# Attention kernel, token stage: inverses of the softmax row sums spread by GpSimd and turned as two 128x128 squares; VectorE's norm and maximum placed between the two statistics instructions of a row

## The chip, the cores and the metric

The kernel runs on one core of one Trainium2 chip. The metric is the time of one execution in microseconds (us), lower is better. TensorE is written PE in the profile (PEld is its loading of weights), VectorE DVE, ScalarE ACT, GpSimd POOL, the queue of the sync engine SP.

## The reference

Three layers are computed on 4 samples of 32x32 pixels with 256 channels (1024 tokens of 256 values each). The middle one is a Nystrom attention with 8 heads of 32 channels and 128 landmarks, and it is there that the change acts:

```python
kernel_1 = softmax(einsum('bhnd,bhmd->bhnm', q, k_l))   # tokens x landmarks
kernel_2 = softmax(einsum('bhmd,bhld->bhml', q_l, k_l)) # landmarks x landmarks
kernel_3 = softmax(einsum('bhmd,bhnd->bhmn', q_l, k))   # landmarks x tokens
pinv = _iterative_pinv(kernel_2)                        # 6 iterations
attn = kernel_1 @ (pinv @ (kernel_3 @ v))
t = t + attn @ w_out.T + b_out                          # attn on _ln_t(t)
t = t + _L1_ffn_ref(_ln_t(t), ...)                      # 16 experts, top 2
```

Ahead of it stands a plain attention over the pixels of a sample, behind it a layer norm and a mixture of 16 experts.

## The kernel before, in words

Everything is in float32. The samples are passed through one after another (variable `i`, 4 passes). A pass has three stages of 8 units each (`UNITS = 3 * NT` = 24, `NT` = 8 row tiles of 128): units 0 to 7 are the plain attention, 8 to 15 the landmark rows with the iterated inverse, 16 to 23 the token stage, which holds `kernel_1` and is where the change acts. After the four passes come the routing and 79 blocks of the experts.

Each engine has its own program, written out by hand; engines meet only at counting semaphores. No scheduler or planner orders the work: what stands first in an engine's code runs first, and an engine that waits holds up all that stands behind it. In the token stage every engine loops over steps `s` = 0 to 9; a tile `t` passes through several steps.

- PE, step `s`: `turn_probs(s)` (8 transposes of the exponentials of tile `s`, L530), `scores(s+2)` (L633), `values(s-1)` (8 matmuls onto 32 partitions each, four column strips of the array side by side, L709), `turn_inverses(s)` (L683), `finish(s-2)` (L723, the output projection). Towards the end stand also transposes of the next sample's input (`turn(16)`, `turn(20)`), and its projections `project_tpg` (L559).
- ACT, step `s`: the exponentials of tile `s+1`, one instruction for each head with the row's sum (L1053), then the copy of the turned exponentials of tile `s` out of PSUM (L1061).
- DVE, step `s`: `inverses(s)` (reciprocal of 8 row sums, L1303), `rows1(s-3)` (adds the residual, L1358, then the two statistics instructions L1324 and L1326 through `moments`), `norm1(s-4)` (L1329), `maxima(s+2)` (L1206), `out_t(s-1)` (L1320), `inverses_turned(s)` (L1307).
- POOL: for each tile, the power -1/2 of the variance (`deviation`, L391 and L392), which `norm1` waits for.

The softmax of `kernel_1` is divided out late. The outputs of `values` have channels on partitions and tokens along the row, so the reciprocals (tokens on partitions, 8 heads along the row) must be turned as well: `turn_inverses` multiplies with `ident`, taking one head's column of `head_inv` 32 times as the weights; 8 matmuls fill PSUM with [32 equal rows for each head x 128 tokens]. `inverses_turned` copies this to `inv_T`, and `out_t` multiplies by it. `turn_inverses(s)` and `values(s-1)` write two halves of one PSUM bank, so `out_t(s-1)` waits for `turn_inverses(s)` (semaphore `inv_mm`). The first waits of `finish(s-2)` are `ot_ready` (from `out_t`) and `pr_used`, which `rows1(s-3)` raises when it has read the bank of the projection.

At the end of a pass DVE has to give the next pass its start as well: `phi_out` (L1212) for the projections, `bulk` (L1194) copies, and `maxima(0)` of the next pass.

Of the kernel before, what the change touches and what calls it, by code (L numbers as in the profile page):

```python
# [5 lines left out]
P = 128  # L6
# [12 lines left out]
QUADS = 4  # L19
# [27 lines left out]
def conv_attn_nystrom_moe_kernel(  # L47
# [34 lines left out]
    with ExitStack() as ctx:  # L82
# [57 lines left out]
        head_inv = sb("head_inv", [P, 2, HEADS])  # L140
        neg_max = sb("neg_max", [P, 2, NT])
# [79 lines left out]
        dve_steps = Chain(sem("dve_steps"), 44)  # L221
# [32 lines left out]
        inv_mm = sem("inv_mm")  # L254
        inv_copied = sem("inv_copied")
# [6 lines left out]
        x2_done = sem("x2_done")  # L262
        dev_ready = sem("dev_ready")
# [104 lines left out]
        def _(pool):  # L368
# [37 lines left out]
            for i in range(B):  # L406
                for t in range(NT + 1):
                    if t < NT:
                        pool.wait_ge(x1_done, i * NT + t + 1)
                        apart(pool, "pool")  # L410
                        deviation(t, i).then_inc(dev_ready, 1)
                    if t >= 1:
                        pool.wait_ge(xn_ready, i * NT + t)
                        pool.tensor_tensor(x1[:, t - 1, :], x1[:, t - 1, :], bo1, ALU.add).then_inc(x1b_ready, 1)
                if i + 1 < B:
                    add_bias(i + 1)
                for t in range(NT):
                    pool.wait_ge(x2_done, i * NT + t + 1)
                    apart(pool, "pool")
                    deviation(t, i).then_inc(dev2_ready, 1)  # L420
                pool_steps.close()
# [112 lines left out]
        def _(pe):  # L534
# [125 lines left out]
            for i in range(B):  # L660
# [13 lines left out]
                def turn_inverses(t):  # L674

                    pe.wait_ge(inv_ready, i * NT + t + 1)
                    if t == 0:

                        pe.wait_ge(pr_used, i * UNITS + 2 * NT)
                    for g in range(NG):  # L680
                        for j in range(QUADS):
                            h = g * GH + j
                            mm = pe.matmul(PS[HD * j:HD * j + HD, 0, g * P:(g + 1) * P], head_inv[:, t % 2, PLACE[h]:PLACE[h] + 1].broadcast_to([P, HD]),  # L683
                                           ident[:], start=True, stop=True, tile_position=(0, HD * j))
                    mm.then_inc(inv_mm, 1)
# [479 lines left out]
        def _(dve):  # L1165
# [128 lines left out]
            for i in range(B):  # L1294
                link = lambda ins: dve_steps.link(dve, ins, i)

                def inverses(t):

                    u = 2 * NT + t
                    dve.wait_ge(s_exp, i * UNITS + u + 1)  # L1300
                    if t >= 2:
                        dve.wait_ge(inv_mm, i * NT + t - 1)
                    dve.reciprocal(head_inv[:, t % 2, :], head_sum[:, u % 2, :]).then_inc(inv_ready, 1)  # L1303
# [47 lines left out]

                def rows1(t):
# [6 lines left out]
                    dve.wait_ge(pr_used, i * UNITS + u + 1)  # L1359
                    apart(dve, "dve")  # L1360
                    moments(t2_row(t), t, x2_done)
# [134 lines left out]
                for s in range(NT + 2):  # L1496
                    if 1 <= s < NT:
                        inverses(s)
                    if s == 0:
# [10 lines left out]
                    if s >= 3:  # L1510
                        rows1(s - 3)
                    if s >= 4:
                        norm1(s - 4)
                    if s + 2 < NT:
                        maxima(2 * NT + s + 2)
                    if 1 <= s < NT:
                        out_t(2 * NT + s - 1)
# [5 lines left out]
                if more:  # L1523
                    phi_out(i + 1, 1)
                norm1(NT - 2)
                if more:
                    bulk(18, xT[:, 0, 0:512])
                    maxima(0, i + 1)
# [166 lines left out]
```

## Time and profile before

| | |
|---|---|
| median of 3 runs | 1000.76 us (999.5, 1000.76, 1002.37) |
| the profiled execution, its own time | 999.48 us |
| its span | 997.3 us |
| PE busy | 908.4 us (91%) |
| PE weight loads busy | 699.0 us (70%) |
| DVE busy | 569.3 us (57%) |
| ACT busy | 448.1 us (45%) |
| POOL busy | 298.6 us (30%) |
| granted PE clock, mean | 0.956 of full speed |
| chain that ended last | PE 73%, DVE 13%, issue 5%, DMA 4%, ACT 3%, POOL 1% |

The span reaches from the first to the last instruction; what lies around it is 2.2 us. The chain is followed back from the last instruction to what released each step. Busy times of matmuls overlap one another, so it is starts that tell the pace: the token stage of the second sample runs from about 293 to 334 us, and those of the others lie at about 138, 444 and 599 us.

### The profile page before, as it was taken

The page shows a single profiled execution, that of the slowest core. Times are in us where ns is not written, and L with a number is a line of the kernel's source. Part 1 is how long each engine was busy: PE and PEld are TensorE (multiplying, and loading weights), DVE is VectorE, ACT ScalarE, POOL GpSimd, SP SyncE. Part 2 cuts the span into 40 slices and gives each one's busy share as a digit, 9 for nine tenths or more (in the row PEclk, how much of TensorE's full clock was granted, in tenths as well). Part 3 has the DMA queues.
Part 4 walks back from the last instruction along what each step waited for, and adds up shares of the span by engine and source line. Part 5 has one row for each costly group of instructions (what it writes and reads, how often), then busy time and mean ns, then how long its engine had stood idle before and what let it go on. Part 6 is the DMA issues. An engine that isn't in the chain of part 4 may idle for free.

```text
span 997.3 us, 21748 instructions
## 1 busy us (share of the span) xinstructions
PE 908.4 (91%) x6980; PEld 699.0 (70%) x6982; DVE 569.3 (57%) x1585; ACT 448.1 (45%) x1004; POOL 298.6 (30%) x343
## 2 busy tenths in 40 slices
PE   5999989899999899999899999546899999999997
PEld 3565767565767565767556767335789999999996
DVE  3478857587857687866678866693222222222221
ACT  1424367433359443349443348253334444444442
POOL 3050001060001050001130000103467666767664
PEclk9699999899999999999899999857999999999999
DMA  3100000300000300000200000499444444444341
GB/s 106 43 2 1 1 2 23 107 1 1 2 1 2 126 3 1 2 1 2 86 1 1 1 2 2 135 252 326 125 67 71 66 69 66 69 65 64 62 65 16
DMA packets 47848, 50.76 MB, mean 51 GB/s; under 512 B 11073, under 2 KB 41153, under 8 KB 47777
## 3 DMA queue, kind: packets, MB, share of 16 engines
q0 software_dynamic: 15168, 18.85, 11.7%
q1 hardware_dynamic: 32608, 30.99, 10.3%
q8 instruction: 42, 0.69, 0.3%
q14 instruction: 30, 0.24, 0.1%
HBM read 33.00 MB, written 18.78 MB: 52 GB/s over the span
## 4 chain that ended last, share of the span: by engine, by line
PE 73%; DVE 13%; issue 5%; DMA 4%; ACT 3%; SPq 1%; POOL 1%; POOLq 0%; DVEq 0%; ACTq 0%
PE PS L982 12%; PE PS L530 11%; PE PS L991 11%; PE PS L851 7%; PE PS L559 6%; PE PS L622 4%; PE PS L723 3%; PE PS L633 3%; PE PS L704 3%; DVE neg_max L1206 3%; DMA out_dram<-low,row_of 3%; PE PS L627 3%; PE PS L709 2%; ACT arena L1053 1%; PE PS L718 1%
## 5 line engine op out<-in xcount | busy, mean ns | idle before, releaser
L391 POOL TENSOR_SCALAR aggr<-aggr 128x1 f32<-128x1 f32 x64 | 14.3, 223 | 519.6 <-DVE aggr L1326 519.6
L1206 DVE TENSOR_REDUCE neg_max<-PS 128x1 f32<-128x1024 f32 (+1 forms) x96 | 117.5, 1224 | 78.2 <-PE PS L633 27.4
L530 PE MATMUL PS<-ident,arena 128*128 128x128 f32 x1008 | 140.3, 287 | 19.8 <-DMA arena<-in_x_dram 6.9
L982 PEld LDWEIGHTS PS<-low 128*128 128x128 f32 x1264 | 155.1, 194 | 4.1
L530 PEld LDWEIGHTS PS<-ident,arena 128*128 128x128 f32 x1008 | 122.7, 150 | 46.9 <-issue 37.7
L982 PE MATMUL PS<-low 128*128 128x128 f32 x1264 | 155.3, 277 | 0.0
L991 PE MATMUL PS<-arena,low 128*128 x632 | 151.9, 384 | 3.3 <-issue 1.6
L439 POOL DMA_INDIRECT out_dram<-low,row_of x79 | 125.4, 1588 | 87.0 <-DVE low L1660 38.6
L1061 ACT COPY arena<-PS 128x1024 f32<-128x1024 f32 x96 | 98.4, 1025 | 92.0 <-PE PS L530 92.0
L991 PEld LDWEIGHTS PS<-arena,low 128*128 128x128 f32 x632 | 114.9, 192 | 18.0 <-issue 5.4
L1149 ACT ACTIVATE low<-PS 128x512 f32<-128x512 f32 x79 | 47.2, 597 | 156.6 <-PE PS L982 156.6
L1048 ACT ACTIVATE arena<-PS,neg_max 128x1024 f32<-128x1024 f32 x64 | 71.3, 1114 | 97.0 <-DVE neg_max L1206 97.0
L425 POOL DMA_INDIRECT low<-rows_scratch,token_of x79 | 78.3, 991 | 65.9 <-DVE token_of L1616 39.4
L1660 DVE TENSOR_SCALAR low<-PS,slot_gate 128x256 f32<-128x256 f32 x79 | 38.2, 483 | 99.8 <-issue 65.0
L1140 ACT COPY low<-arena 128x1024 f32 x79 | 82.5, 1045 | 28.2 <-issue 28.2
L1053 ACT ACTIVATE arena<-PS,neg_max 128x128 f32<-128x128 f32 x256 | 90.4, 399 | 7.6 <-DVE neg_max L1206 7.6
L1641 DVE TENSOR_TENSOR gate_parts<-low,pick_of 128x2 f32<-128x2 f32 x79 | 12.7, 161 | 129.6 <-PE PS L530 129.6
L851 PE MATMUL PS<-arena 128*128 128x256 f32 x320 | 74.4, 386 | 0.0
L559 PE MATMUL PS<-arena,low 128*128 128x512 f32 x128 | 63.6, 622 | 4.5 <-DVE arena L1460 2.6
L851 PEld LDWEIGHTS PS<-arena 128*128 128x128 f32 x320 | 59.1, 190 | 11.2 <-issue 4.0
L1053 ACT ACTIVATION_READ_ACCUMULATOR arena<-PS,neg_max 128x1 f32 x256 | 60.9, 238 | 0.0
L1025 ACT ACTIVATE arena<-PS 128x512 f32<-128x512 f32 x40 | 23.7, 596 | 81.9 <-PE PS L559 40.2
(203 smaller groups left out, 1312.2 us busy)
## 6 DMA issues: line engine op xcount, KB each, us to landing
arena<-in_L_ffn_W_dram SPq DMA_DIRECT2D x32, 512.0 KB, 5.7
arena<-in_x_dram SPq DMA_DIRECT2D x4, 1024.0 KB, 6.4
out_dram<-t SPq DMA_DIRECT2D x4, 1024.0 KB, 6.8
rows_scratch<-arena SPq DMA_DIRECT2D x4, 512.0 KB, 3.7
rows_scratch<-arena SPq DMA_DIRECT2D x8, 256.0 KB, 2.6
low<-rows_scratch,token_of POOLq DMA_INDIRECT x79, 2.9
out_dram<-low,row_of POOLq DMA_INDIRECT x79, 3.8
arena<-in_L_attn_w_qkv_dram SPq DMA_DIRECT2D x1, 768.0 KB, 4.8
```

Source lines behind the costliest of these rows:

```text
L425: pool.indirect_dma_start(xg[:, n % 4, :], None, rows_dram, bass.IndirectOffsetOnAxis(ap=token_of[:, n:n + 1], axis=0)).then_inc(xg_loaded ...
L439: pool.indirect_dma_start(out_rows, bass.IndirectOffsetOnAxis(ap=row_of[:, n:n + 1], axis=0), y_sb[:, n % 4, :], None, bounds_check=T - 1, ...
L530: mm = pe.transpose(PS[0:s.shape[1], dst_bank, n * P:n * P + s.shape[0]], s, ident[0:s.shape[0], 0:s.shape[0]])
L559: mm = pe.matmul(PS[0:m, bank, :], w[c], src[:, c, half * 512:half * 512 + 512], start=c == 0, stop=c == KC - 1)
L851: mm = pe.matmul(bank[:, o:o + 2 * M], RX[:, g, h, 0, :], RX[:, g, h].rearrange("p r m -> p (r m)"), start=True, stop=True)
L982: mm = pe.matmul(PS[:, 2 + p, hc * P:(hc + 1) * P], w1_now[:, p, c * H + hc * P:c * H + (hc + 1) * P], xgT[:, p, c, :], start=c == 0, stop ...
L991: mm = pe.matmul(PS[:, 6 + p, 0:D], hT[:, p, c, :], w2_sb[:, bass.ds(e * (HC * D) + c * D, D)], start=c == 0, stop=c == HC - 1)
L1048: act.activation(Pm[:, u % 2, :], src, ACT.Exp, bias=neg_max[:, u % 2, 0:1], accum_out=row_sum[:, u % NT:u % NT + 1]).then_inc(s_exp, 1)
L1053: ins = act.activation(Pm[:, u % 2, o:o + M], src[:, o:o + M], ACT.Exp, bias=neg_max[:, u % 2, h:h + 1], accum_out=head_sum[:, u % 2, h:h ...
L1061: act.copy(PT[:, u % 2, :], PS[:, 2:4, :].rearrange("p b n -> p (b n)")).then_inc(t_act, 1)
L1140: act.copy(w1_now[:, p, :], w1_sb[:, bass.ds(e * (KC * H), KC * H)]).then_inc(w1_staged, 1)
L1206: dve.tensor_reduce(dst, src, AX.X, ALU.max, negate=True).then_inc(s_max, 1)
```

## The change

Two parts.

1. `turn_inverses` no longer multiplies. A new buffer `inv_spread` (128 x 2 x 256) is filled by POOL (`spread_inverses`): two copies per tile write each head's reciprocal 32 times side by side. PE then turns the two 128x128 squares with two transposes. POOL waits for `inv_ready`, PE for the new semaphore `inv_spread_ready`, and `inverses(t)` waits for POOL's reading of tile `t-2`. POOL's `deviation(t-3)` stands behind `spread_inverses(t)`.
2. On DVE the row statistics are taken apart: `rows1` only adds, `stats1` and `moments1` are functions of their own. In a step `rows1` and `norm1` come first, then `stats1`, `maxima`, `moments1`; `bulk(20)` and the last `out_t` now stand behind `rows1` and `norm1`, and in the last steps `phi_out` stands ahead of `stats1`.

```diff
+                def spread_inverses(t):
+                    pool.wait_ge(inv_ready, i * NT + t + 1)
+                    if t >= 2:
+                        pool.wait_ge(inv_mm, i * NT + t - 1)
+                    by_place = head_inv[:, t % 2, :].rearrange("p (a g b) -> p g a b", g=NG, b=2)
+                    for g in range(NG):
+                        pool.tensor_copy(inv_spread[:, t % 2, g * P:(g + 1) * P].rearrange("p (a b d) -> p a b d", a=2, b=2),
+                                         by_place[:, g].unsqueeze(3).broadcast_to([P, 2, 2, HD])).then_inc(inv_spread_ready, 1)
+
+                for t in range(NT + 3):
+                    if t < NT:
+                        spread_inverses(t)
+                    if t >= 3:
+                        pool.wait_ge(x2_done, i * NT + t - 3 + 1)
+                        apart(pool, "pool")
+                        deviation(t - 3, i).then_inc(dev2_ready, 1)
...
-                    pe.wait_ge(inv_ready, i * NT + t + 1)
+                    pe.wait_ge(inv_spread_ready, (i * NT + t + 1) * NG)
-                    for g in range(NG):
-                        for j in range(QUADS):
-                            h = g * GH + j
-                            mm = pe.matmul(PS[HD * j:HD * j + HD, 0, g * P:(g + 1) * P], head_inv[:, t % 2, PLACE[h]:PLACE[h] + 1].broadcast_to([P, HD]),
-                                           ident[:], start=True, stop=True, tile_position=(0, HD * j))
-                    mm.then_inc(inv_mm, 1)
+                    transposes(pe, 0, [inv_spread[:, t % 2, g * P:(g + 1) * P] for g in range(NG)]).then_inc(inv_mm, 1)
...
                 for s in range(NT + 2):
                     if 1 <= s < NT:
                         inverses(s)
+                    if s >= 3:
+                        rows1(s - 3)
+                    if s >= 4:
+                        norm1(s - 4)
...
                     if s >= 3:
-                        rows1(s - 3)
-                    if s >= 4:
-                        norm1(s - 4)
+                        stats1(s - 3)
                     if s + 2 < NT:
                         maxima(2 * NT + s + 2)
+                    if s >= 3:
+                        moments1(s - 3)
```

The order on DVE in a middle step of the token stage (from the reciprocal to `out_t`; `t2` holds the rows after the attention, and `arena` in the norm is the buffer `xn`), before:

```order
L1303 RECIPROCAL head_inv<-head_sum 128x8 [waits inv_mm,s_exp]
L1358 TENSOR_TENSOR t2<-PS,arena 128x256 [waits x1b_ready,pr_mm]
L1324 BN_STATS stats<-t2 128x6 [waits pr_used]
L1326 BN_AGGR aggr<-stats 128x2 [waits dve_steps]
L1329 TENSOR_SCALAR arena<-t2,aggr 128x256 [waits dev2_ready]
L1206 TENSOR_REDUCE neg_max<-PS 128x8 [waits s_exp,s_mm]
L1320 TENSOR_TENSOR low<-PS,arena 128x256 [waits inv_copied,inv_mm,pr_mm,pv_mm]
```

and now:

```order
L1315 RECIPROCAL head_inv<-head_sum 128x8 [waits inv_spread_ready,s_exp]
L1380 TENSOR_TENSOR t2<-PS,arena 128x256 [waits x1b_ready,pr_mm]
L1341 TENSOR_SCALAR arena<-t2,aggr 128x256 [waits dev2_ready]
L1367 BN_STATS stats<-t2 128x6 [waits pr_used]
L1218 TENSOR_REDUCE neg_max<-PS 128x8 [waits s_exp,s_mm]
L1372 BN_AGGR aggr<-stats 128x2 [waits x2_stats]
L1332 TENSOR_TENSOR low<-PS,arena 128x256 [waits inv_copied,inv_mm,pr_mm,pv_mm]
```

The norm has moved ahead of the statistics, and the maximum between the two statistics instructions; nothing is added or taken away.

On PE at the same step, from `values` to `finish`, before:

```order
L709 MATMUL PS<-arena,low 32x128 [waits inv_copied,ot_ready,t_act]
L709 MATMUL PS<-arena,low 32x128 x7
L683 MATMUL PS<-ident,head_inv 32x128 [waits inv_ready]
L683 MATMUL PS<-ident,head_inv 32x128 x7
L723 MATMUL PS<-low 128x256 [waits pr_used,ot_ready]
L723 MATMUL PS<-low 128x256
```

and now:

```order
L721 MATMUL PS<-arena,low 32x128 [waits inv_copied,ot_ready,t_act]
L721 MATMUL PS<-arena,low 32x128 x7
L547 MATMUL PS<-ident,inv_spread 128x128 [waits inv_spread_ready]
L547 MATMUL PS<-ident,inv_spread 128x128
L735 MATMUL PS<-low 128x256 [waits pr_used,ot_ready]
L735 MATMUL PS<-low 128x256
```

The eight matmuls onto 32 partitions are two transposes onto 128, and they wait for POOL in place of DVE.

On POOL, for two tiles in the middle of the stage, now (before, only the pairs on `aggr` stood there):

```order
L428 COPY inv_spread<-head_inv 128x128 [waits inv_mm,inv_ready]
L428 COPY inv_spread<-head_inv 128x128
L394 TENSOR_SCALAR aggr<-aggr 128x1 [waits x2_done]
L395 TENSOR_TENSOR aggr<-aggr,minus_half 128x1 [waits pool_steps]
L428 COPY inv_spread<-head_inv 128x128 [waits inv_mm,inv_ready]
L428 COPY inv_spread<-head_inv 128x128
```

The two copies of a tile stand behind the deviation that the step before asked for, and ahead of the one of its own step.

On DVE at the end of the stage, from the last-but-one `out_t` on, before:

```order
L1320 TENSOR_TENSOR low<-PS,arena 128x256 [waits inv_copied,inv_mm,pr_mm,pv_mm]
L1307 COPY arena<-PS 128x256 [waits inv_mm]
L1194 COPY arena<-PS 128x512 [waits bulk_mm]
L1320 TENSOR_TENSOR low<-PS,arena 128x256 [waits inv_copied,pr_mm,pv_mm]
L1358 TENSOR_TENSOR t2<-PS,arena 128x256 [waits x1b_ready,pr_mm]
L1324 BN_STATS stats<-t2 128x6 [waits pr_used]
L1326 BN_AGGR aggr<-stats 128x2 [waits dve_steps]
L1329 TENSOR_SCALAR arena<-t2,aggr 128x256 [waits dev2_ready]
```

and now:

```order
L1332 TENSOR_TENSOR low<-PS,arena 128x256 [waits inv_copied,inv_mm,pr_mm,pv_mm]
L1319 COPY arena<-PS 128x256 [waits inv_mm]
L1380 TENSOR_TENSOR t2<-PS,arena 128x256 [waits x1b_ready,pr_mm]
L1341 TENSOR_SCALAR arena<-t2,aggr 128x256 [waits dev2_ready]
L1206 COPY arena<-PS 128x512 [waits bulk_mm]
L1332 TENSOR_TENSOR low<-PS,arena 128x256 [waits inv_copied,pr_mm,pv_mm]
L1367 BN_STATS stats<-t2 128x6 [waits pr_used]
L1372 BN_AGGR aggr<-stats 128x2 [waits x2_stats]
```

The addition L1358 (now L1380), which raises `pr_used`, stood behind the copy of 512 and the last `out_t`; now it stands ahead of both, and the norm directly behind it.

## Rows read from the trace of the kernel before

**Rows 1.** Chain that ended last, second sample, a middle step: start us, us, what

```profile
311.71 0.57 PE PS L709 x16
312.29 0.44 PE PS L683 x16
312.72 1.06 PE PS L723 x4
313.78 0.87 PE PS L530 x8
314.66 1.06 PE PS L633 x8
```

**Rows 2.** Timeline, DVE, same step: start us, us, engine, line, operation [idle before <-releaser]

```profile
311.76 1.22 DVE L1206 TENSOR_REDUCE neg_max<-PS 128x8 f32<-128x1024 f32 x1 [0.33 <-PE PS L633]
...
312.90 0.41 DVE L1320 TENSOR_TENSOR low<-PS,arena 128x256 f32<-128x256 f32 x1
...
313.56 0.19 DVE L1303 RECIPROCAL head_inv<-head_sum 128x8 f32<-128x8 f32 x1
...
314.39 0.43 DVE L1324 BATCH_NORM_STATS2 stats<-t 128x6 f32<-128x256 f32 x1
...
314.96 0.18 DVE L1326 BATCH_NORM_AGGREGATE aggr<-stats 128x2 f32<-128x6 f32 x1
...
315.77 1.22 DVE L1206 TENSOR_REDUCE neg_max<-PS 128x8 f32<-128x1024 f32 x1 [0.33 <-PE PS L633]
```

**Rows 3.** Timeline, ACT, second sample: first exponential of two tiles that follow each other

```profile
301.26 0.44 ACT L1053 ACTIVATE arena<-PS,neg_max 128x128 f32<-128x128 f32 x1
...
305.00 0.40 ACT L1053 ACTIVATE arena<-PS,neg_max 128x128 f32<-128x128 f32 x1
```

**Rows 4.** POOL: a copy of 128x128 (ns min/median/max), and the deviation's second instruction (timeline)

```profile
L405 POOL COPY wk_turned<-low x4: 285/290/293, 23.7 to 24.4; 128x128 f32<-128x128 f32 x4
...
315.65 0.57 POOL L392 TENSOR_TENSOR aggr<-aggr,minus_half 128x1 f32<-128x1 f32 x1
```

**Rows 5.** Timeline, PE, expert blocks: two transposes, and what follows them

```profile
866.79 0.38 PE L530 MATMUL PS<-ident,low 128*128 128x128 f32 x2
867.00 1.89 PE L991 MATMUL PS<-arena,low 128*128 x8
```

**Rows 6.** Timeline, PE, start of the third pass: two transposes ahead of matmuls onto 32 partitions

```profile
345.73 0.44 PE L602 MATMUL PS<-ident,arena 128*128 128x128 f32 x2
346.09 0.64 PE L704 MATMUL PS<-arena,low 128*32 128x128 f32 x16
```

**Rows 7.** Timeline, PE and DVE, end of the second sample's token stage

```profile
326.97 1.10 PE L723 MATMUL PS<-low 128*128 128x256 f32 x4 [0.97 <-DVE t L1358]
...
332.21 1.04 PE L530 MATMUL PS<-ident,arena 128*128 128x128 f32 x8
...
332.52 0.76 DVE L1212 TENSOR_SCALAR arena<-PS,bias_col 32x512 f32<-32x512 f32 x1
...
334.59 1.23 DVE L1206 TENSOR_REDUCE neg_max<-PS 128x1 f32<-128x1024 f32 x1
```

**Rows 8.** Timeline, PE and DVE, end of the last sample's token stage

```profile
627.08 1.06 PE L530 MATMUL PS<-ident,arena 128*128 128x128 f32 x8 [0.24 <-ACT arena L1061]
...
637.14 0.41 DVE L1329 TENSOR_SCALAR arena<-t,aggr 128x256 f32<-128x256 f32 x1 [0.81 <-POOL aggr L392]
```

**Rows 9.** Windows: us, busy PE PEld DVE ACT POOL (x), granted PE clock, DMA, GB/s

```profile
184.00:188.00 4.00, 4.00 (x14) 2.17 (x13) 1.30 (x2) 1.01 (x1) 0.00 (x0) 0.50 0.02 4
336.00:340.00 4.00, 2.80 (x19) 1.91 (x20) 2.17 (x4) 3.16 (x5) 0.00 (x0) 1.00 0.20 70
```

**Rows 10.** Timeline, PE: first turning of inverses in passes one, two and three

```profile
142.46 0.64 PE L683 MATMUL PS<-ident,head_inv 128*32 128x128 f32 x16
...
297.02 0.64 PE L683 MATMUL PS<-ident,head_inv 128*32 128x128 f32 x16
...
448.44 0.64 PE L683 MATMUL PS<-ident,head_inv 128*32 128x128 f32 x16
```

More of the change, by code:

```diff
@@ L140, in conv_attn_nystrom_moe_kernel @@
         head_inv = sb("head_inv", [P, 2, HEADS])
+        inv_spread = sb("inv_spread", [P, 2, D])
         neg_max = sb("neg_max", [P, 2, NT])
@@ L220, in conv_attn_nystrom_moe_kernel @@
         dve_chain0 = Chain(sem("dve_chain0"))
-        dve_steps = Chain(sem("dve_steps"), 44)
+        dve_steps = Chain(sem("dve_steps"), 36)
         dve_chain2 = Chain(sem("dve_chain2"))
@@ L254, in conv_attn_nystrom_moe_kernel @@
         inv_mm = sem("inv_mm")
+        inv_spread_ready = sem("inv_spread_ready")
         inv_copied = sem("inv_copied")
@@ L262, in conv_attn_nystrom_moe_kernel @@
         x2_done = sem("x2_done")
+        x2_stats = sem("x2_stats")
         dev_ready = sem("dev_ready")
@@ L416, in _ @@
                     add_bias(i + 1)
[L417 to L420, printed above, removed]
+                def spread_inverses(t):
[13 more added lines that the diff above has]
+                        deviation(t - 3, i).then_inc(dev2_ready, 1)
                 pool_steps.close()
@@ L1301, in inverses @@
                     if t >= 2:
-                        dve.wait_ge(inv_mm, i * NT + t - 1)
+                        dve.wait_ge(inv_spread_ready, (i * NT + t - 1) * NG)
                     dve.reciprocal(head_inv[:, t % 2, :], head_sum[:, u % 2, :]).then_inc(inv_ready, 1)
@@ L1350, in rows0, with stats1, moments1 @@
                     moments(x1[:, t, :], t, x1_done)
+                def stats1(t):
+                    dve.wait_ge(pr_used, i * UNITS + 2 * NT + t + 1)
+                    dve.bn_stats(stats[:, 0:6], t2_row(t)).then_inc(x2_stats, 1)
+                def moments1(t):
+                    dve.wait_ge(x2_stats, i * NT + t + 1)
+                    dve.bn_aggr(aggr[:, t, 0:2], stats[:, 0:6]).then_inc(x2_done, 1)
                 def rows1(t):
@@ L1358, in rows1 @@
                     dve.tensor_tensor(t2_row(t), PS[:, 1, 0:D], x1[:, t, :], ALU.add).then_inc(pr_used, 1)
-                    dve.wait_ge(pr_used, i * UNITS + u + 1)
-                    apart(dve, "dve")
-                    moments(t2_row(t), t, x2_done)
                 maxima(1)
@@ L1524, in _ @@
                     phi_out(i + 1, 1)
+                stats1(NT - 1)
                 norm1(NT - 2)
+                moments1(NT - 1)
                 if more:
```

## The prediction

> **What bounds the kernel now.** I read the chain that ended last first, then the timeline of one middle step of the token stage, engine by engine, then the end of the stage. The chain through a middle step is PE alone [rows 1]: values 0.57 us, turning of the inverses 0.44, output projection 1.06, turning of the exponentials 0.87, scores 1.06. That is 4.00 us, and the maximum on DVE comes back every 315.77 - 311.76 = 4.01 us [rows 2]. So PE never waits here, and DVE waits 0.33 us for PE's scores in each step. ACT is close behind: where nothing held it, it went from the first exponential of one tile to that of the next in 305.00 - 301.26 = 3.74 us [rows 3]. DVE needs 4.01 - 0.33 = 3.68 us. Three engines stand within 8% of one another; what PE gives up is worth 0.27 us a step at most, then ACT sets the pace. At the end of the stage the order on DVE counts: PE waits 0.97 us for the addition L1358 of a tile three behind [rows 7].
>
> **What PE gains in a step.** Removed are 8 matmuls onto 32 partitions (16 records), 0.44 us of the chain [rows 1]. Added are two transposes. Eight of them take 0.87 us in the chain [rows 1], so two take 0.22; in the expert blocks two are followed by the next group after 867.00 - 866.79 = 0.21 us [rows 5]. I take a gain of 0.44 - 0.22 = **0.22 us**. The ends: two transposes next to matmuls onto 32 partitions took 346.09 - 345.73 = 0.36 us [rows 6], which leaves a gain of 0.08; ACT's 3.74 us caps it at 0.27.
>
> **Where that gain counts.** Tiles are turned at steps 0 to 7. At steps 0 and 1 ACT is the pace (its 3.74 us between tiles is from there [rows 3]), so I count nothing. Steps 2 to 7 count in the first three passes: 6 x 0.22 = 1.32 us. In the last pass nothing of a next sample stands between the transposes, and PE waits 0.24 us for ACT's copy at the last tile [rows 8]. ACT there has moved forward only by what reached it through the scores, those of steps 2 to 4; the gains of steps 5 and 6 go into that wait. So 3 x 0.22 and the one of step 7: 0.88 us.
>
> **What DVE gains in a middle step.** Before, from the start of the first statistics instruction to the start of the second it is 314.96 - 314.39 = 0.57 us, of which 0.43 is work: 0.14 us of handover [rows 2]. The maximum between the two now covers it, and the norm covers that from the addition to the statistics. DVE has about 0.3 us less to do in a step that it spent waiting for PE anyway: nothing for the sum, but it keeps DVE (some 3.4 us) under the new pace of 3.79 us.
>
> The new order has a price of its own: the norm of a tile now comes before the next statistics, and waits for GpSimd. The deviation was done 315.65 + 0.57 - 314.96 = 1.26 us after the second statistics instruction began [rows 2, 4]; about 0.04 more to DVE. That instruction now starts where out_t started, 312.90 - 311.76 = 1.14 us after the maximum, so the norm may start 2.44 us after it. DVE gets there when the addition is done, where the first statistics instruction stood before: 314.39 - 311.76 = 2.63 us, less its handover of 0.14, and 0.1 later for the second statistics instruction, so 2.6. It just fits; a miss of a few tenths goes into the slack of 0.4 us ahead of the maximum.
>
> **What GpSimd adds.** Two copies of 128x128 in a tile; the trace has the same size at 0.29 us [rows 4], with a plain source instead of a repeated one. The reciprocal ends 313.56 + 0.19 - 311.76 = 2.0 us after the maximum starts [rows 2], GpSimd is busy with the deviation to 2.44, so the squares are ready at 2.44 + 0.58 and about 0.1 for the handover: 3.1 us. PE wants them in the next step, after values: 3.79 + 0.57, less 0.06 from scores to maximum, 4.3 us. The margin is 1.2 us, and a copy could take 0.9 before PE waits. From below a copy costs nothing, from above I take the 0.57 us of the deviation's second instruction [rows 4]; I go by 0.29, the row of the same size, and both ends are hidden by the work that PE has until then.
>
> The Trainium skill (SBUF — State Buffer, section "SBUF: two separate sides") says that VectorE and GpSimd take one pair of SBUF ports as an exclusive lock for a whole instruction, if VectorE's is in a two-port mode or reads two SBUF operands. By it each copy could stand still behind a norm, 0.41 us in [rows 8], and the squares would be ready at some 3.9 us instead of 3.1: still before 4.3, so the sum is the same by it, but most of the margin is gone. No row of before has such a copy beside a norm.
>
> **The end of the stage, first three passes.** The addition that PE waited for now stands ahead of the copy of 512 and of the last out_t, right behind the projection that it reads. The wait of 0.97 us [rows 7] goes; PE is then 1.32 + 0.97 = 2.29 us early at the projections of the next sample. phi_out follows them: before, it began 332.52 - 332.21 = 0.31 us after PE had gone on [rows 7], about 0.15 of that because the statistics stood ahead of it; it gains 2.4. But between phi_out and the next pass's first maximum (334.59 - 332.52 = 2.07 us before [rows 7]) there are now both statistics instructions of the last tile, 0.43 + 0.18 [rows 2], overlapped about 0.4 us. The first maximum, on which the next pass hangs, comes 2.29 + 0.15 - 0.4 = **2.05 us** earlier. Three passes: 6.15 us.
>
> **The end of the last pass.** PE's 0.88 us and a wait like the 0.97 of [rows 7] go. What is late next is the norm: with only the addition between the second statistics instruction and the norm, DVE now stands and waits for the 1.26 us of GpSimd, tile by tile (before, one such wait of 0.81 us was left, before the last norm [rows 8]). I walked through the three remaining tiles with the durations of [rows 2, 4]: the last norm, at 637.14 before, comes about 0.1 us earlier by this part, so **1.0 us** with PE's. Behind it routing and experts follow unchanged.
>
> **The sum.** 6.15 + 1.0 = 7.15 us. From the profiled execution, 999.48 us (span 997.3 and 2.2 around it), that gives 992.3; the median shown is 1.3 us above that execution, so the forecast is 1000.8 - 7.2 = **993.6 us**. With the gain in a step at 0.08 the sum is 7.15 - 22 x 0.14 = 4.1 us (22 tiles counted), with 0.27 it is 8.2.
>
> **The rivals.**
>
> *The clock takes part of it.* After the change of passes PE ran at a granted 0.50, the lower level of 1.2 GHz, in 184 to 188 us, and at 1.00, 2.4 GHz, in the same place of the next pass, 336 to 340, where it was busy for 2.80 of 4 us, in a pause for the first exponentials [rows 9]. The price: the first pass to the second is 297.02 - 142.46 = 154.56 us, the second to the third 448.44 - 297.02 = 151.42 [rows 10], 3.1 us for one such stretch. The first maximum gains less (2.05) than PE's scores (2.4), so PE's pause there grows by some 0.4 us. One stretch more: 993.6 + 3.1 = 996.7, 15%. One fewer: 990.5, 10%. The Trainium skill (TensorE: Matmul & The Clock Gate, "What's actually happening") has the activity window running free of the kernel, and the trace agrees in so far as the two changes of passes of [rows 9] show two levels; by it a shift of a few us draws anew in every pass, and the time would be one of the two just given.
>
> *ACT or a chain of waits swallows the step's gain.* For it: ACT has only 0.27 us to give [rows 2, 3]. Against: its exponentials hang on the maximum, and that moves forward with the scores. Then only the ends of the stages gain, 3 x (0.97 + 0.15 - 0.4) + 0.1 = 2.3 us: 998.5, no change. 10%.
>
> *Slower: GpSimd is late.* If a copy with a repeated source takes 1.5 us instead of 0.29, PE's turning waits, and through out_t, which waits for it, DVE and ACT. The loop from one maximum to the maximum two tiles on is 2.44 + 0.1 to the copies, then the two copies, 0.22 for the turning, 1.06 + 0.87 + 1.06 for projection, transposes and scores, 0.06 to the maximum: 5.8 us and two copies, and it must fit into two steps. Up to 0.9 us a copy nothing happens, from 1.1 us the step is as long as before (2 x 4.01), at 1.5 it is 4.4 us: 0.39 x 22 = 8.6 us lost, 2.3 gained at the ends, 1007 us. For it speaks only that no repeated source stands in the rows, against it the 0.29 [rows 4]. 4%.
>
> *The new order on DVE does nothing at the ends*, because the norm, now ahead of the copy of 512, waits for GpSimd and brings the old wait back: 6 x 0.22 each and 0.9, 4.9 us in all, 995.9. For it: the norm needs a deviation asked for only some 2 us before. Against: at step 8 it is the deviation of a tile whose statistics ended ahead of the out_t of step 7, two DVE instructions, the addition and a wait for PE earlier. 10%.
>
> **Chances.** Forecast as it stands, 991.5 to 996: 51%; nothing at the ends 10%; clock one more 15%, one fewer 10%, swallowed 10%, late 4%. A measurement of this kernel tells about 0.3%, 3 us, from no change. Faster by more (under 997.8): 51 + 10 + 15 + 10 = 86, less 2 for the upper edge of the clock's case, 84%; within: 12%; slower: 4%. With ACT as the cap and one stretch fewer the sum reaches 989.5, with one stretch more or a gain of 0.08 in a step it ends at 996.7; the range from 989.7 to 997.2 leaves out the two last rivals and the edges.
>
> **What would show it.** The maximum on DVE every 3.8 us in the middle of the stage, PE without a pause; two transposes followed by the projection after 0.22 us; copies on GpSimd of about 0.3 us that end a microsecond before PE's turning; no wait of PE for the addition at the end of the stage; the next pass's first exponentials 2 us earlier relative to the start of this one's token stage. Wrong would be: a pace of 4.0 us with ACT or GpSimd as the releaser, squares that PE waits for, or a third stretch at a clock of 0.50.

## The result and the profile after

The changed kernel took 993.5 us in the median of 8 runs (989.46 to 995.29), the kernel before 997.81 in 8 runs (996.04 to 1002.37; the first three of them are the ones shown above). The ratio is 0.9941, with a 95% interval of 0.9917 to 0.9965: faster by 0.6%, or 5.9 us (3.5 to 8.3). The means differ by that much (998.5 and 992.5 us); the medians differ by 4.3 us. Forecast were 993.6 us and 7.2 us less.

The profiled execution took 990.14 us, its span is 988.3. Busy times changed little:

```profile
PE 899.4 (91%) x6533; PEld 690.7 (70%) x6534; DVE 564.5 (57%) x1585; ACT 447.0 (45%) x1004; POOL 315.8 (32%) x407
```

The chain that ended last, through a middle step of the second sample (start us, us, what), answers to [rows 1]:

```profile
303.52 0.57 PE PS L721 x16
304.10 0.37 PE PS L547 x2
304.47 0.87 PE PS L735 x4
305.33 0.87 PE PS L547 x8
306.21 1.06 PE PS L650 x8
```

It is still PE alone, and the step is 3.74 us instead of 4.00. The two transposes (L547, 0.37) are not as cheap as forecast, 0.07 us under the eight matmuls; but the projection behind them (L735) takes 0.87 instead of 1.06. Together they are 1.24 us, against 0.44 + 1.06 = 1.50: 0.26 us gained. The timeline of PE in the same step:

```profile
303.45 0.64 PE L721 MATMUL PS<-arena,low 128*32 128x128 f32 x16
304.03 0.44 PE L547 MATMUL PS<-ident,inv_spread 128*128 128x128 f32 x2
304.31 1.03 PE L735 MATMUL PS<-low 128*128 128x256 f32 x4
305.17 1.04 PE L547 MATMUL PS<-ident,arena 128*128 128x128 f32 x8
```

From start to start the transposes take 304.31 - 304.03 = 0.28 us, and the matmuls of `values` in front of them 304.03 - 303.45 = 0.58, where it was 0.46 before:

```profile
311.64 0.65 PE L709 MATMUL PS<-arena,low 128*32 128x128 f32 x16
312.10 0.62 PE L683 MATMUL PS<-ident,head_inv 128*32 128x128 f32 x16
312.65 1.13 PE L723 MATMUL PS<-low 128*128 128x256 f32 x4
```

The chain counts from the end of what stands in front, and so puts that difference to the transposes.

DVE in the same step, from the timeline (compare [rows 2]):

```profile
303.57 1.22 DVE L1218 TENSOR_REDUCE neg_max<-PS 128x8 f32<-128x1024 f32 x1 [0.58 <-PE PS L650]
304.71 0.17 DVE L1372 BATCH_NORM_AGGREGATE aggr<-stats 128x2 f32<-128x6 f32 x1
304.80 0.39 DVE L1332 TENSOR_TENSOR low<-PS,arena 128x256 f32<-128x256 f32 x1
...
305.99 0.41 DVE L1341 TENSOR_SCALAR arena<-t,aggr 128x256 f32<-128x256 f32 x1
306.32 0.42 DVE L1367 BATCH_NORM_STATS2 stats<-t 128x6 f32<-128x256 f32 x1
307.32 1.22 DVE L1218 TENSOR_REDUCE neg_max<-PS 128x8 f32<-128x1024 f32 x1 [0.58 <-PE PS L650]
```

The maximum comes back after 3.75 us. DVE waits longer for PE than before (0.58 us against 0.33) although the step is shorter: its own part fell from 3.68 to 3.17 us. The norm (L1341) has no wait in front of it. It stands ahead of both statistics instructions, and not between them as the title has it.

POOL, timeline:

```profile
305.08 0.22 POOL L394 TENSOR_SCALAR aggr<-aggr 128x1 f32<-128x1 f32 x1 [2.27 <-DVE aggr L1372]
305.39 0.57 POOL L395 TENSOR_TENSOR aggr<-aggr,minus_half 128x1 f32<-128x1 f32 x1
305.91 0.65 POOL L428 COPY inv_spread<-head_inv 128x128 f32<-128x128 f32 x2
```

The squares are ready at 306.56, and PE turns them at 307.78: 1.2 us of margin, as reckoned. That holds only where scores stand ahead of the turning. At step 6 there are none left to do, PE comes 1.06 us sooner, and the margin is 310.46 - (309.65 + 0.65) = 0.16 us:

```profile
309.65 0.65 POOL L428 COPY inv_spread<-head_inv 128x128 f32<-128x128 f32 x2
310.46 0.44 PE L547 MATMUL PS<-ident,inv_spread 128*128 128x128 f32 x2
```

The end of the stage, PE and DVE (compare [rows 7]):

```profile
316.77 1.13 PE L735 MATMUL PS<-low 128*128 128x256 f32 x4
...
322.35 0.76 DVE L1224 TENSOR_SCALAR arena<-PS,bias_col 32x512 f32<-32x512 f32 x1 [1.16 <-PE PS L576]
...
324.61 1.21 DVE L1218 TENSOR_REDUCE neg_max<-PS 128x1 f32<-128x1024 f32 x1
...
327.21 1.94 PE L547 MATMUL PS<-ident,arena 128*128 128x128 f32 x8 [1.97 <-ACT arena L1060]
```

The projection L735 has lost its wait of 0.97 us. The last row shows two things more: PE's pause ahead of the new pass is 1.97 us, and the eight transposes behind it take 1.94 us, about twice as long as elsewhere (1.04 to 1.10). The window that follows is at the lower clock:

```profile
328.00:332.00 4.00, 4.00 (x15) 2.17 (x14) 0.74 (x1) 1.53 (x3) 0.00 (x0) 0.50 0.02 4
```

**Where the time went.** The multiplication of Y at step 0 (L1501 before, L1524 after, the DVE instruction of 128x256 from PS and small) marks each token stage. In the traces of all kernels below, its starts, the start of the last norm and that of the first expert matmul (L982 before) divide the span. All columns are us worked out from those starts; "stage" is from Y to the last norm of the same sample in passes one to three. "Filled" kernels have useless transposes in PE's pauses, and the "other tail" is another order on DVE at the end of the stage; both are described under Experiments:

| kernel | start to first Y | pass 1, 2, 3 | stage | last stage | then to experts | experts to end | span |
|---|---|---|---|---|---|---|---|
| before | 138.7 | 154.6, 151.4, 154.7 | 42.49 | 37.8 | 47.3 | 312.8 | 997.3 |
| before again | 136.8 | 154.6, 151.4, 156.2 | 42.49 | 37.8 | 47.7 | 313.9 | 998.4 |
| after | 136.4 | 149.2, 152.2, 153.9 | 40.16 | 36.4 | 48.1 | 312.2 | 988.3 |
| transposes alone | 138.2 | 154.8, 153.2, 153.1 | 41.00 | 36.9 | 48.2 | 312.6 | 997.0 |
| order alone | 138.3 | 154.0, 153.8, 153.9 | 41.66 | 37.4 | 47.5 | 313.2 | 998.0 |
| after, filled | 136.6 | 149.2, 149.0, 149.0 | 40.18 | 36.5 | 47.7 | 313.8 | 981.8 |
| after, filled, again | 136.5 | 149.2, 149.0, 149.0 | 40.17 | 36.4 | 47.6 | 313.8 | 981.6 |
| before, filled | 139.4 | 151.4, 151.3, 151.3 | 42.48 | 37.8 | 46.5 | 313.8 | 991.5 |
| after, other tail | 138.4 | 155.0, 152.2, 154.9 | 40.09 | 35.7 | 48.2 | 314.5 | 998.9 |
| other tail, filled | 136.6 | 149.0, 148.8, 148.8 | 40.09 | 35.7 | 47.6 | 311.8 | 978.4 |
| other tail, all filled | 131.7 | 149.0, 148.8, 148.8 | 40.09 | 35.7 | 46.4 | 315.8 | 976.2 |

Two of the marks of the changed kernel as rows of its timeline; 285.58 - 136.36 = 149.2:

```profile
136.36 0.42 DVE L1524 TENSOR_TENSOR low<-PS,small 128x256 f32<-128x256 f32 x1 [3.42 <-PE PS L906]
285.58 0.42 DVE L1524 TENSOR_TENSOR low<-PS,small 128x256 f32<-128x256 f32 x1 [3.43 <-PE PS L906]
```

The stage is the same to 0.03 us in every pass and trace of a kernel, filled or not. A whole pass is not: 151.4 us before where the clock was full, and 3 to 6 us more, over all kernels, where a stretch of 0.50 fell into its start. The start is not either (136.4 to 139.4 where its pause is not filled): two projections early in it (L559 before, 11 us in) took 3.67 us in some executions and 5.5 to 6.1 in others, the kernel before among the former in its second trace. Its first trace and its second:

```profile
11.40 5.55 PE L559 MATMUL PS<-arena,low 128*128 128x512 f32 x8 [0.88 <-issue]
```

```profile
11.35 3.67 PE L559 MATMUL PS<-arena,low 128*128 128x512 f32 x8 [1.08 <-DVE arena L1194]
```

The granted clock reads 1.00 there in both traces, so the cause of the difference is not shown.

### The profile page after: what moved, and what is told of

It reads as the page before. It is cut to its first block, busy times and chain, and to the rows that moved or that the text cites. A ratio compares the mean times of both kernels' runs of the same rounds, so it can differ in the third digit from the quotient of the medians.

```text
span 988.3 us, 20877 instructions
## 1 busy us (share of the span) xinstructions
PE 899.4 (91%) x6533; PEld 690.7 (70%) x6534; DVE 564.5 (57%) x1585; ACT 447.0 (45%) x1004; POOL 315.8 (32%) x407
## 3 DMA queue, kind: packets, MB, share of 16 engines
q1 hardware_dynamic: 32608, 30.99, 10.1%
## 4 chain that ended last, share of the span: by engine, by line
PE 71%; DVE 13%; issue 5%; ACT 5%; DMA 3%; POOL 1%; SPq 1%; POOLq 0%; DVEq 0%; ACTq 0%
PE PS L994 12%; PE PS L1003 12%; PE PS L547 12%; PE PS L863 7%; PE PS L576 6%; PE PS L639 3%; PE PS L716 3%; DVE neg_max L1218 3%; PE PS L644 3%; PE PS L650 3%; ACT arena L1065 2%; PE PS L735 2%; DMA out_dram<-low,row_of 2%; ACT arena L1073 2%; PE PS L721 1%
## 5 line engine op out<-in xcount | busy, mean ns | idle before, releaser
L547 PE MATMUL PS<-ident,arena 128*128 128x128 f32 x1008 | 141.0, 288 | 23.3 <-ACT arena L1073 7.5
L547 PEld LDWEIGHTS PS<-ident,arena 128*128 128x128 f32 x1008 | 123.4, 151 | 50.3 <-issue 39.2
L994 PE MATMUL PS<-low 128*128 128x128 f32 x1264 | 154.9, 276 | 0.0
L428 POOL COPY inv_spread<-head_inv 128x128 f32<-128x128 f32 x64 | 18.3, 315 | 325.5 <-DVE head_inv L1315 325.5
L576 PE MATMUL PS<-arena,low 128*128 128x512 f32 x128 | 61.7, 606 | 4.7 <-DVE arena L1479 2.6
```

Of the source, the lines that this page charges most:

```text
L547: mm = pe.transpose(PS[0:s.shape[1], dst_bank, n * P:n * P + s.shape[0]], s, ident[0:s.shape[0], 0:s.shape[0]])
L576: mm = pe.matmul(PS[0:m, bank, :], w[c], src[:, c, half * 512:half * 512 + 512], start=c == 0, stop=c == KC - 1)
L994: mm = pe.matmul(PS[:, 2 + p, hc * P:(hc + 1) * P], w1_now[:, p, c * H + hc * P:c * H + (hc + 1) * P], xgT[:, p, c, :], start=c == 0, stop ...
```

## Experiments

**The transposes alone.** The first part of the change alone, the kernel before with `inv_spread`, `spread_inverses` and two transposes; DVE's order is that of before.

```diff
+ pool: spread_inverses(t); deviation(t - 3)
- pe: 8 matmuls, head_inv column broadcast x ident
+ pe: transposes(pe, 0, [inv_spread[:, t % 2, g * P:(g + 1) * P] for g in range(NG)])
  dve: rows1 + bn_stats + bn_aggr, norm1, maxima   (as before)
```

> The first part of the change alone: GpSimd spreads the inverses and TensorE turns two squares; VectorE's order is that of before. Theory A (the step was bound by TensorE, the end of the stage by VectorE's order, and the two parts act in different places): the maximum comes back every 3.75 us in the middle of the stage instead of 4.01, the wait of TensorE for the addition at the end of the stage stays at about 1.0 us, and a pass from its first turning of exponentials in the token stage to that of the next pass's first unit takes 44.17 - 6 x 0.26 = 42.6 us. In all about 6 us less than before. Rival B (VectorE's order is what allows the faster step, since with its old order it has 3.68 us of work and handovers and stands in the way): the step stays near 4.0 or lands at 3.9, and less than 3 us are gained.

Measured: 997.43 us, ratio to before 0.9962 (0.9942 to 0.9982), which is 3.8 us less where about 6 were expected. The step is 3.75 us with the old order on DVE, so rival B falls. The stage is 1.49 us shorter, the last 0.9. PE's wait for the addition is there to the hundredth:

```profile
325.26 1.10 PE L733 MATMUL PS<-low 128*128 128x256 f32 x4 [0.97 <-DVE t L1368]
```

In this trace each of the three passes had a stretch at the lower clock, where the traces of the kernel before had two. That may be why less was gained than the 3 x 1.49 + 0.9 = 5.4 us of the stages; one trace does not show it for the median.

**The order alone.** The changed kernel with the eight matmuls and POOL's old loop put back.

```diff
- pool: spread_inverses(t)
- pe: transposes(pe, 0, ...)
+ pe: 8 matmuls, head_inv column broadcast x ident
  dve: rows1, norm1, stats1, maxima, moments1   (as changed)
```

> The second part alone: VectorE's new order, with the eight matmuls of before. Theory A: the step stays at 4.01 us, TensorE's wait for the addition at the end is gone, the stage up to the next pass is 44.17 - 0.8 = 43.4 us, and the whole is 2 to 3 us faster than before, which one median can hardly tell from no change. Rival B (VectorE's order carries the step): the step falls below 3.9 us and 5 us or more are gained.

Measured: 1000.31 us, ratio 1.0 (0.9985 to 1.0016). DVE's maxima stay 4.01 us apart:

```profile
310.82 1.23 DVE L1208 TENSOR_REDUCE neg_max<-PS 128x8 f32<-128x1024 f32 x1 [0.84 <-PE PS L635]
314.83 1.23 DVE L1208 TENSOR_REDUCE neg_max<-PS 128x8 f32<-128x1024 f32 x1 [0.84 <-PE PS L635]
```

What DVE saved in a step became wait, 0.84 us instead of 0.33. The stage is 0.83 us shorter, and the last one 0.5. Of the 3 x 0.83 + 0.5 = 3.0 us nothing can be seen in the time, where 2 to 3 were expected. In the trace three stretches of lower clock, where the traces of the kernel before had two, took as much as was gained; that this holds for the median is not shown. The two parts add up: 1.49 + 0.83 = 2.32 us a stage, and together they gave 42.49 - 40.16 = 2.33.

**A shorter copy on ScalarE.** Is it still PE that sets the step? This kernel leaves out half of the copy, so half of the heads are computed from stale values; it serves for its trace alone.

```diff
-act.copy(PT[:, u % 2, :], PS[:, 2:4, :]...)
+w = 512 if u >= 2 * NT else 1024
+act.copy(PT[:, u % 2, 0:w], PS[:, 2:4, :]...[:, 0:w])
```

> The changed kernel with ScalarE's copy of the turned exponentials in the token stage cut to half its columns (half of the heads are left stale), so that ScalarE has about 0.4 us less in a step. Theory A (TensorE still sets the step, at 3.75 us): the step stays at 3.74 to 3.75 us and TensorE shows no pause in steps 2 to 7; only steps 0 and 1 become shorter, TensorE's wait of 1.37 us for the copy shrinks by 0.4. Rival G (ScalarE, whose own pace was 3.74 us before, has become the bound): the step falls by 0.2 us or more.

Measured (one run, 988.12 us): the step stays at 3.74 to 3.75. ACT now waits, where in the changed kernel it did not:

```profile
310.95 0.37 ACT L1065 ACTIVATE arena<-PS,neg_max 128x128 f32<-128x128 f32 x1 [0.37 <-DVE neg_max L1219]
```

PE's one wait for ACT, at step 2, fell from 1.37 to 0.95 us, which is most of the 0.5 us by which the stage fell. So PE is the bound of the middle steps; ACT, without a wait at the same 3.74 us, is level with it.

**More copies on GpSimd.** Two or six copies into an unread buffer ahead of the two that count.

```diff
+for n in range(2):          # 6 in the second kernel
+    pool.tensor_copy(unread[:, t % 2, n]..., by_place[:, 0].unsqueeze(3).broadcast_to([P, 2, 2, HD]))
 for g in range(NG):
     pool.tensor_copy(inv_spread[...], ...)
```

> The changed kernel with two more copies of 128x128 on GpSimd ahead of the two that count, into a buffer that nobody reads. Theory A (the squares are ready more than a microsecond before TensorE wants them): the squares come 0.65 us later and nothing else moves, the step stays at 3.75 us. Rival H (GpSimd is already on the path, hidden in a short wait): the step grows by 0.2 us or more.

> The same with six more copies, 2 us of GpSimd's time in a tile. Theory A with its margin of 1.2 us: TensorE now waits for the squares, the step is 4.2 to 4.3 us, longer than the 4.01 of the kernel before, and the time is 10 to 14 us above the changed kernel. Rival (the loop over GpSimd has far more room than the margin says): step under 3.9 us.

With two (one run, 994.68 us) the step stays at 3.75 us, but the expected "nothing else moves" is wrong: at step 6, where the margin was 0.16 us, PE waits, and the stage is 40.44 us instead of 40.16:

```profile
313.76 0.44 PE L551 MATMUL PS<-ident,inv_spread 128*128 128x128 f32 x2 [0.30 <-POOL inv_spread L432]
```

With six (one run, 998.67 us) PE waits for the squares, 0.18 us at step 4 and 1.25 at step 6, but the distances of the maxima are 3.75, 3.74, 4.00, not 4.2 to 4.3:

```profile
308.99 0.44 PE L551 MATMUL PS<-ident,inv_spread 128*128 128x128 f32 x2 [0.18 <-POOL inv_spread L432]
...
316.73 0.44 PE L551 MATMUL PS<-ident,inv_spread 128*128 128x128 f32 x2 [1.25 <-POOL inv_spread L432]
```

The six copies took 1.47 to 1.59 us, some 0.3 more than the margin of 1.2, and PE waited 0.18: the margin of a middle step is confirmed. Most of the price was paid at step 6, where the margin is the short one, and no longer step stood in the stage than the 4.00. It cost 41.64 - 40.16 = 1.5 us a stage, and the time was 5 us above that of the changed kernel where 10 to 14 were expected.

**Filling the pause.** 16 transposes of the identity in PE's pause at the start of each pass but the first; nobody reads their result.

```diff
 turn_g(i)
 bulk_done(19, i - 1)
+for _ in range(16):
+    transposes(pe, 2, [ident[:]])
```

> The changed kernel with 16 transposes of the identity added at each start of a pass but the first, in TensorE's pause of 2 us before the first exponentials are there; their result is read by nobody and is overwritten. Theory C (the stretches at a granted clock of 0.50 at the changes of passes come from that pause): no window between 170 and 500 us shows less than 1.00, each of the two stretches of the changed kernel gives back its 3 us, and the kernel is 4 to 6 us faster than the changed one. Rival D (they come from somewhere else, or the transposes delay the start by more than they save): the stretches stay, and the time is that of the changed kernel or 1 us above it.

Measured: 984.45 us (982.84 to 985.21), ratio 0.9839 (0.9816 to 0.9863). The changed kernel stands at 0.9941, so the filling is worth some 10 us. No window of the three changes of passes shows less than 1.00, and all three passes are 149.0 to 149.2 us. Theory C holds, with about twice the gain expected. It does so with the kernel before too:

> The kernel before with the same 16 added transposes at each start of a pass but the first. Theory C (the pause at the start of a pass brings the clock down, in the kernel before too): no window between 170 and 500 us under 1.00, every pass 151.4 us long, 3 to 9 us faster than before. Rival: it has no effect on the kernel before, whose pause is 0.2 us shorter.

> The changed kernel with the 16 transposes, taken again beside the one above. With the clock held in both, their difference is that of the change alone. By the traces it is 3 x 2.34 us at the changes of passes and 1.4 us at the end of the last, 8.4 us in all, less at most 0.5 behind it. If instead it is under 6 us, the change costs something outside the token stage that the lengths of its passes do not show.

Measured on one chip: the kernel before, filled, 992.2 us (991.15 to 993.71), ratio 0.9916 (0.9891 to 0.9941), and the changed one, filled, 982.1 us (978.48 to 983.33), ratio 0.9812 (0.9785 to 0.984). The window in which the changed kernel stood at 0.50, now of the changed kernel filled, and the same place of the kernel before filled:

```profile
328.00:332.00 4.00, 4.00 (x27) 2.39 (x25) 1.82 (x2) 3.09 (x6) 0.00 (x0) 1.00 0.11 9
```

```profile
332.00:336.00 4.00, 4.00 (x32) 3.01 (x30) 3.01 (x4) 2.36 (x5) 0.00 (x0) 1.00 0.20 70
```

With the clock held in both kernels the change is worth 10.1 us between the medians. The traces account for 8.1 inside the token stages and their turns (2.2 + 2.3 + 2.3 in the passes, 1.3 at the end); their starts differ by 3.0 more, 2.5 of it in the two projections named above (6.14 and 3.67 us), and 1.1 go the other way behind the last norm, where PE's next work fell at a clock of 0.59 in the changed kernel and of 1.00 in the one before.

**Another tail.** Norm behind both statistics at step 9, and the last tile's statistics ahead of the second `phi_out`.

```diff
-if s >= 4:
+if 4 <= s < NT + 1:
     norm1(s - 4)
...
     moments1(s - 3)
+if s == NT + 1:
+    norm1(s - 4)
...
 rows1(NT - 1)
-if more: phi_out(i + 1, 1)
 stats1(NT - 1)
-norm1(NT - 2)
 moments1(NT - 1)
+norm1(NT - 2)
+if more: phi_out(i + 1, 1)
```

> The changed kernel with another order on VectorE in the last two steps and behind them: the norm behind both statistics instructions again in step 9, and the last tile's statistics and the norm ahead of the second phi_out, where VectorE stood idle for 1.16 us. Theory E (what the new order gave back at the end of the stage is the statistics and the norm between phi_out and the next pass's first maximum): that maximum comes 0.8 us earlier after phi_out, three times, and the last norm 0.3 us earlier; 2.7 us less than the changed kernel. Rival F (the first maximum waits for TensorE's scores anyway): less than 0.3 us a pass, no change.

Measured: 994.73 us (988.61 to 1000.77), ratio 0.9932 (0.9906 to 0.9958), no difference from the changed kernel. The 12 runs fall in two groups, five of 988.6 to 990.2 us with a mean granted clock of 0.955 to 0.958, and seven of 994.1 to 1000.8 at 0.942 to 0.948: what spreads the time of one and the same kernel goes with the clock. Rival F holds for the turn of the passes: the first maximum now waits for PE's scores,

```profile
332.29 1.23 DVE L1218 TENSOR_REDUCE neg_max<-PS 128x1 f32<-128x1024 f32 x1 [0.59 <-PE PS L639]
```

and with the clock held a pass is 148.8 us instead of 149.0. The last stage became 0.8 us shorter, where 0.3 were expected.

**Both, and all pauses filled.** The first kernel has the other tail and the 16 transposes. The second fills two more pauses of PE:

```diff
 scores(0, k)
+keep_warm(34, bank=7)       # start, while DVE copies the weights
...
+keep_warm(24, bank=4)       # last pass, ahead of turn_high(B - 1)
 turn_high(B - 1)
```

> The other order at the end of the stage and the 16 added transposes together. If theories C and E both hold: 6 to 8 us faster than the changed kernel, about 986 us. If the pause is shorter by the better order, the 16 transposes (1.75 us) may delay the first turning of exponentials by up to 0.5 us a pass, and 1.5 us of it are lost again.

> The other order at the end of the stage, the 16 transposes, and two more fills of TensorE's pauses: 34 transposes while the weights are copied at the start, 24 ahead of the last half of the rows' turning in the last pass. If a pause of 4 us at the start is what brings the clock down there for 20 us, the first pass becomes 5 to 8 us shorter; at the end about 1 us. In all 6 to 9 us faster than the same kernel without the two fills (978.9 us). Rival: the fall at the start has another cause, and only the 1 us at the end is gained.

Measured: 978.87 us, ratio 0.9799 (0.9776 to 0.9822), and 975.38 us, ratio 0.975 (0.9721 to 0.978). The first is well below the 986 us expected, since the filling was worth more; the second gained 3.5 us on it by the medians and 4.9 by the ratios, less than the 6 to 9 expected. The second shortened the start by 4.9 us to 131.7, and the way from the last norm to the experts by 1.3. Its two early projections took 5.63 us in this trace, in the first kernel's 3.67; against the other tail unfilled, where they took 5.76, the start is 138.4 - 131.7 = 6.7 us shorter. In the window 24 to 28 us of the start the changed kernel and the filled one read:

```profile
24.00:28.00 4.00, 4.00 (x14) 2.07 (x12) 1.23 (x1) 2.11 (x3) 0.00 (x0) 0.50 0.00 0
```

```profile
24.00:28.00 4.00, 3.44 (x20) 1.61 (x18) 1.69 (x3) 0.94 (x1) 0.49 (x3) 1.00 0.00 0
```

It is the fastest of all, 2.5% under the kernel before. Its stretch of experts, at 315.8 us, was the longest of the table; it lies between 311.8 and 315.8 over kernels that have the same code there.

**The kernel before once more.**

> The kernel before once more, for a second trace of it. If the first token stage's start at 138.7 us (136.5 in six of the eight traces that hold both parts of the change) belongs to the kernel, it is 138 to 139 again; if it is drawn anew in each execution, by the clock that TensorE is granted in the first 12 us, it may as well be 136.5. The undisturbed pass is 151.4 us; with a stretch of lower clock 154.5 or more, and how many of the three passes have one may differ from the first trace.

Measured: 999.24 us. The start was 136.8 us, so it differs from execution to execution and is no merit of the change. Two of the three passes had a stretch, of 3.2 and 4.8 us.

## Why the prediction was right, point by point

**PE bounds the step, ACT is next.** Right. The shortened copy on ScalarE shows it: no faster step.

**0.22 us a step.** The size was a little low: 0.26. The transposes cost 0.37 us and not 0.22, so the row of two transposes beside matmuls onto 32 partitions, 0.36 [rows 6], was nearer than that of the expert blocks. Both rows were read from start to start, and by that measure it is 0.28 now, between the two, with 0.12 more for the matmuls in front. What the term left out is that the projection behind them fell from 1.06 to 0.87, as it does wherever it follows instructions on all 128 columns (0.86 behind L576 at the end of the stage). The place where PE goes over from the one form to the other moved, from ahead of the projection to ahead of the transposes.

**Steps 0 and 1 give nothing.** Right: from the first maximum after Y to the third it was 4.58 + 3.94 = 8.52 us before and is 4.07 + 4.45 = 8.52 now; PE's wait for ACT grew from 0.80 to 1.37.

**GpSimd's copies are hidden, margin 1.2 us.** Right in the middle steps: 0.315 us a copy in the mean, ready 1.2 us early. Wrong for step 6: the sum of 3.79 + 0.57 us has the scores in it, and without their 1.06 us the prediction's own figures leave 4.3 - 1.06 - 3.1, or 0.1 to 0.2 us; measured are 0.16. So the copies cost nothing as they are, but a copy could not take 0.9 us before PE waits, and two more already cost 0.28 us a stage. The rule of the Trainium skill (SBUF — State Buffer, section "SBUF: two separate sides") is borne out in direction only: a pair of copies took 0.52 us where it ran alone and 0.65 where the norm began 0.08 us behind it, 0.13 us more in a tile and not up to 0.8; where the norm began 0.18 us behind a pair, the norm took 0.49 us instead of 0.38 to 0.42. Whether the norm is of the kind that the rule speaks of, no run shows. The rows of the second case:

```profile
311.96 0.52 POOL L428 COPY inv_spread<-head_inv 128x128 f32<-128x128 f32 x2 [0.19 <-DVE head_inv L1315]
312.14 0.49 DVE L1341 TENSOR_SCALAR arena<-t,aggr 128x256 f32<-128x256 f32 x1
```

**DVE's order gives nothing in the step.** Right: alone it left the step at 4.01 and raised DVE's wait to 0.84. The norm, which was to start 2.6 us after the maximum and "just fit", started at 2.42, 0.03 after the deviation had ended.

**2.05 us at each turn of the passes, 1.0 at the end.** Right in kind, low in size: 2.33 and 1.4. Of 2.33, 1.49 came with the transposes alone (forecast 1.32) and 0.83 with the order (forecast 0.72). At the end the transposes alone gave 0.9 (forecast 0.88) and the order 0.5 (forecast 0.1): the three norms waited 0.61, 0.32 and 1.10 us for GpSimd, less than the walk assumed. The sum of the terms is 8.4 us instead of 7.15. Two rivals fall by this: the step did get shorter, so nothing swallowed its gain, and the order alone took 0.83 us off each stage, so it did something at the ends.

**The clock.** It was named as a rival with a price of 3.1 us a stretch, one more or one fewer. The mechanism is there: filling the pause brought 8.4 us to the kernel before (ratio 0.9916), more than two stretches at 3.1. A stretch cost 3.2 to 4.8 us in the two traces of the kernel before, 3.1 and 4.9 in that of the changed one, and up to 6 with the other tail. The number of stretches was two in all three traces; PE's pause grew by 0.2 us (1.79 to 1.97), not by 0.4. In the changed kernel the filling brought 10.2 and 12.9 us (0.9839 and 0.9812 against 0.9941). By these medians and ratios the clock took 2 to 4.5 us more from the changed kernel than from the one before, which would leave 4 to 6.5 us of the 8.4 that the terms add up to, about the 5.9 measured. The intervals of these ratios overlap, so this part is likely and not shown.

**The number.** That 993.6 was forecast and 993.5 measured is luck. The forecast was taken from a median of 1000.8 us, but over its 8 runs the kernel before stood at 997.8 (and at 999.2 to 1000.4 in later sets), so the base was 3 us too high; the gain was 4.3 us by the medians and 5.9 by the means, not 7.2. And that 5.9 is near 7.2 rests on two errors against one another: terms too low by 1.2 us, and, as far as is known, a loss to the clock that the likeliest case had not in it.

## What to carry to other kernels

Cut work on the engine that the chain runs through, and pay for it on an engine with a margin that can be read as a distance in time between the end of its work and the start of what waits for it; here 0.63 us on GpSimd bought 0.26 on TensorE. Read that margin at every step of the loop, the last ones too: it was 1.2 us in the middle and 0.16 where the scores had run out. Price a group of matmuls with the one behind it: what follows a change of form costs more, and the change moves when the form does. And look at TensorE's granted clock behind each pause: here 16 useless transposes in a pause of 2 us gave 8.4 us to the kernel before and 10 to 13 to the changed one, as much as the change itself, which is 5.9 us as measured and 10.1 with the clock held in both.

## What the runs showed of the hardware

A pause of 1.8 to 2.0 us of PE was followed by 0.50 in some passes and by 1.00 in others of the same execution; in the six unfilled traces of the table 15 of 18 turns of passes had a stretch of 0.50. Filled with transposes no turn had one, in 15 turns of five traces. The two projections 11 us into the program took 3.67 us or 5.5 to 6.1 from execution to execution, at a granted clock that reads 1.00 in both cases; that is worth 2 to 2.5 us in the start. A transpose of 128x128 in float32 takes 0.109 us in a row of eight, and 0.19 in a pair behind matmuls onto 32 partitions, both by the chain. GpSimd's copy of 128x128 with a repeated source is as fast as a plain one: 0.293 us in the median of the 64 records, 0.290 the plain one of [rows 4]; in a row of six a copy took 0.25 to 0.27.
